# Edge stage of a graph layer: four normalised tiles stored as two interleaved pairs, read at a stride of 8 bytes instead of 16

## Chip, cores and metric

The kernel runs on one core of one Trainium2 chip. The metric is device time in microseconds from start to end of one execution. Before the change it is 1327.7 us, the median of three runs (1327.56 to 1327.87).

## What is computed

One graph layer over 100000 nodes of 160 features (64 scalars, then 32 vectors of 3) and 25000 edges. Cut to what matters:

```python
h = jnp.maximum(_layernorm(x, axis=-1), 0.0)      # normalise, relu
s, v = h[:, :64], h[:, 64:].reshape(N, 32, 3)
skip_s, skip_v = s @ W_skip0, einsum('nmi,mk->nki', v, W_skip1)
s, v = s @ W_nl0, einsum('nmi,mk->nki', v, W_nl1)
w = relu(edge_feature @ W_fc1) @ W_fc2            # 224 weights per edge
xs, xv = s[dst], v[dst]                           # rows of each edge
tp = products of w, xs, xv and the edge's direction
agg = segment_sum(tp, src) / 32
out_s = agg_s @ W_out_s + skip_s;  out_v = agg_v @ W_out_v + skip_v
out = x + concat(silu(out_s[:, :64]), sigmoid(out_s[:, 64:96]) * out_v)
```

## The kernel before, in words

The host stores each node's vector part component by component, so that a row is 64 scalars and three blocks of 32. The program is written per engine, with semaphores between them, in three stages:

1. **Table stage** (about 0 to 195 us): for each tile of 125 edges TensorE counts, and VectorE, ScalarE and GpSimd work out, in which slot of its target block each message will be found.
2. **Edge stage** (about 200 to 600 us): 200 tiles of 125 edges in 50 groups of `GE` = 4. GpSimd gathers the four tiles' rows of `x` (`gathers`, L501) three groups ahead. VectorE takes their statistics (L642), GpSimd the power -1/2 (L508), VectorE the shift (L656). ScalarE normalises (`norm_e`, L1093) from `xg` into `hn`. TensorE transposes `hn` (`turn_rows`, L1334 and L1335), ScalarE copies the result out of PSUM into `ht` (L1150), TensorE multiplies it by the weights (`rows`, L1289 and L1293) and the edge features by theirs (L1386, L1378). VectorE forms the products (`products`, L794 to L818) with a part on GpSimd (L562, L564). TensorE transposes them (`turn`, L1349), ScalarE copies them out (L1138), TensorE projects them (`project`, L1362 to L1366), ScalarE copies the messages out (L1145), VectorE completes them (L827 to L831) and SP stores them.
3. **Node stage** (about 600 us to the end): for each 1024 nodes the normalisation (L1178), transposes (L1411, L1412), skip products (L1419, L1423), the sum of gathered messages (L1433), gates and residual. It has a tile `nn` of its own, which the change does not touch.

**The tile of the change.** `hn` is `[125, 2, 160, 4]` in float32: two buffers, in each 160 features, and innermost the four tiles of a group. So one tile's features lie 16 bytes apart. ScalarE writes a tile at that stride, once per tile. TensorE transposes features 0 to 127 of each tile apart (L1334, four times a group, stride 16 bytes), and the last 32 features of all four tiles together: they lie in 128 neighbouring elements (L1335, once a group, no stride). In a transpose the tile is the stationary operand, the one that the weight load (PEld) reads, and the identity is streamed.

**What the weights have to match.** Row p of `ht[:, c, t]` is feature p of tile t; its product with `wnl_a` (128x128: `W_nl0` in the scalars' place, `W_nl1` twice for two vector components) is done per tile. Row p of `ht[:, c, 4]` is feature 128 + p // 4 of tile p % 4; `wnl_z` has `W_nl1` at rows j, j + 4, ... for tile j.

**The order of work.** Each engine's order is written out by hand in a loop over groups, `round_e(q, b)`. One round of TensorE is:

```python
turn(1); project(0); weights((0, 2)); turn(2); project(1)
weights((1, 3)); turn(3); project(2)
turn_rows(q + 1, 1 - c)      # waits for e_norm, the fourth tile of hn
project(3); turn(0, p + 1, 1 - c); rows(p_x, c); hidden of q + 1
```

and in ScalarE's round the two places where `hn` is written are:

```python
take(1); norm_e(q + 1, (b + 1) % D, range(0, 2))
take(2); put(q - 2, c, 0)    # L1145, waits for project(1)
norm_e(q + 1, (b + 1) % D, range(2, 4)); take(3); copy of w (L1168)
```

`take` is L1138, `put` is L1145. At the start of the program VectorE clears the tiles that hold weights (L609), and then SP issues the loads of all weights one after the other (L404), the first loads of edge features (L414) and of `x` (L427). TensorE waits for the weights before L1273, VectorE at line 735, after the table stage.

Of the kernel before, what the change touches and what calls it, by code (L numbers as in the profile page):

```python
# [6 lines left out]
ACT = mybir.ActivationFunctionType  # L7
# [6 lines left out]
P = 128  # L14
# [3 lines left out]
def gnn_layer(nc, x, src, dst, edge_vec, edge_feat_t, w_skip0, w_skip1, w_nl0, w_nl1,  # L18
# [11 lines left out]
    N, F = x.shape  # L30
    S = w_skip0.shape[0]
    V = w_skip1.shape[0]
    SG = w_skip0.shape[1]
# [5 lines left out]
    ET, NT = src.shape  # L39
    GE = 4  # L40
# [24 lines left out]
    with ExitStack() as ctx:  # L65
        def sb(name, shape, dt=F32):
            return ctx.enter_context(nc.sbuf_tensor(name, shape, dt))

        def sem(name):
            return ctx.enter_context(nc.semaphore(name))  # L70
# [46 lines left out]

        wsk_a = sb("wsk_a", [P, SG + 2 * V])
        wsk_z = sb("wsk_z", [P, 4 * V])
        wnl_a = sb("wnl_a", [P, S + 2 * V])  # L120
        wnl_z = sb("wnl_z", [P, 4 * V])
        wfc1 = sb("wfc1", [2 * EF, 2 * EF])
        wfc2 = sb("wfc2", [2 * EF, W])
# [37 lines left out]
        with ExitStack() as msg_ctx:  # L161
            def sb_msg(name, shape, dt=F32):
                return msg_ctx.enter_context(nc.sbuf_tensor(name, shape, dt))


            dst_g = sb_msg("dst_g", [P, D, GE], I32)
            xg = sb_msg("xg", [P, D, GE, F])
            ef = sb_msg("ef", [2 * EF, 2, 2 * ET])
            e_stat = sb_msg("e_stat", [ET, D, GE, 6])
            e_sum = sb_msg("e_sum", [ET, D, 5, GE])  # L170
            e_rstd = sb_msg("e_rstd", [ET, D, GE])
            e_bias = sb_msg("e_bias", [ET, D, GE])
            hn = sb_msg("hn", [ET, 2, F, GE])
            ht = sb_msg("ht", [P, 2, GE + 1, ET])
            hid = sb_msg("hid", [2 * EF, 2 * ET])
            w_sb = sb_msg("w_sb", [ET, 2, GE, W])
            tp = sb_msg("tp", [ET, 2, GE, 2 * TU])
            xvh = sb_msg("xvh", [ET, GE, 3, V])
            dot = sb_msg("dot", [ET, 2, GE, V])
            w4xv = sb_msg("w4xv", [ET, GE, 3, V])  # L180
            cr_a = sb_msg("cr_a", [ET, GE, 3, V])
            cr_b = sb_msg("cr_b", [ET, GE, 3, V])
            tpt = sb_msg("tpt", [P, 2, 3 * ET])
# [62 lines left out]
        e_t = sem("e_t")  # L246
# [47 lines left out]
        weight_loads = [(wfc2[0:EF, :], w_fc2), (wfc2[EF:2 * EF, :], w_fc2)]  # L294
        for j in range(2):
# [1 line left out]
            weight_loads.append((wfc1[part, part], w_fc1))  # L297
        weight_loads += [(wo_s[:, :], w_out_s), (wo_u[S:2 * S, V:2 * V], w_out_v[0:S, :]),
                         (wo_u[0:2 * V, 0:V], w_out_v[S:S + 2 * V, :]),
                         (wsk_a[0:S, 0:SG], w_skip0), (wnl_a[0:S, 0:S], w_nl0)]  # L300
        for j in range(2):
            weight_loads.append((wo_v[2 * V * j:2 * V * j + 2 * V, V * j:V * j + V], w_out_v[S:S + 2 * V, :]))
            rows = slice(S + V * j, S + V * j + V)
            weight_loads += [(wsk_a[rows, SG + V * j:SG + V * j + V], w_skip1),
                             (wnl_a[rows, S + V * j:S + V * j + V], w_nl1)]
        for j in range(4):
            cols = slice(V * j, V * j + V)
            weight_loads += [(wsk_z[j:P:4, cols], w_skip1), (wnl_z[j:P:4, cols], w_nl1)]

        def wait(eng, s, value):  # L310

            if not (isinstance(value, int) and value <= 0):
                eng.wait_ge(s, value)
# [54 lines left out]
        with ExitStack() as psum_ctx:  # L368
# [9 lines left out]
            p_t = bank[0][:, 0:(GE + 1) * P].rearrange("p (t c) -> p t c", c=P)[:, :, 0:ET]  # L378
# [7 lines left out]
            f_t = bank[3][:, 0:(GE + 1) * P].rearrange("p (t c) -> p t c", c=P)[:, :, 0:ET]  # L386
# [699 lines left out]
            def _(act):  # L1086
                act.wait_ge(s_tab, 1)
                act.activation(vec_r[:], vec_d2[:], ACT.Sqrt).then_inc(s_sqrt, 1)
                def norm_e(q, b, tiles):
                    act.wait_ge(e_ln, q + 1)  # L1090
                    wait(act, e_t, q - 1)
                    for t in tiles:
                        last = act.activation(hn[:, b % 2, :, t], xg[0:ET, b, t, :], ACT.Relu,  # L1093
                                              bias=e_bias[:, b, t:t + 1], scale=e_rstd[:, b, t:t + 1])
                    if GE - 1 in tiles:
                        last.then_inc(e_norm, 1)
# [3 lines left out]
                def tile_b(t, k, q):  # L1100
                    if k % BATCH < BATCH - 1:
                        done, s = (BR - BR // BATCH) * q + k - k // BATCH, (k - k // BATCH) % 2
                        act.wait_ge(b_dec, BR // BATCH * q + k // BATCH + 1)
                        act.activation(off_slot[:, s, :], iota_slot[0:ET, :], ACT.Abs, bias=slot[:, k:k + 1],  # L1104
                                       scale=-1.0).then_inc(b_off, 1)
                        wait(act, b_tab, t - BLOCK + 1)
                        act.wait_ge(b_off, done + 1)
                        r = k % BLOCK
                        act.activation(slot_v[:, r, :], off_slot[:, s, :], ACT.Relu, bias=row_no[:, r:r + 1],
                                       scale=neg_row[:, r:r + 1]).then_inc(b_slot, 1)  # L1110
                    if isinstance(t, int) and t == BR - 1:
                        norm_e(0, 0, range(GE))
                    if isinstance(t, int) and t == NT - BR:
                        act.wait_ge(e_t, 1)
                        act.activation(ht[:, 0, :, :], f_t, ACT.Copy).then_inc(e_ht, 1)
                    if isinstance(t, int) and t == NT - BR + 8:
                        act.wait_ge(e_h1, 1)
                        act.activation(hid[:], f_h, ACT.Relu).then_inc(e_hid, 1)
                    if isinstance(t, int) and t == NT - 3:
                        act.wait_ge(e_w, 1)  # L1120
                        act.activation(w_sb[:, 0, :, :], f_w, ACT.Copy).then_inc(e_wsb, 1)
# [3 lines left out]
                for r in range(2):  # L1125
                    last = act.activation(tab_row[:, r, :], p_tab[r], ACT.Copy, scale=unit_of_slot[:, 0:1])
                last.then_inc(b_rows_sb, 1)

                def round_e(q, b):
# [28 lines left out]
                    if within(q + 1):  # L1158
                        norm_e(q + 1, (b + 1) % D, range(0, 2))
                    take(2)  # L1160
                    put(q - 2, c, 0)
                    if within(q + 1):
                        norm_e(q + 1, (b + 1) % D, range(2, 4))
# [73 lines left out]
            def _(pe):  # L1237
# [22 lines left out]

                idt = ident[0:ET, 0:ET]

                def turn_first():
                    pe.wait_ge(e_norm, 1)
                    for t in range(GE):
                        pe.transpose(f_t[:, t, :], hn[:, 0, 0:P, t], idt)
                    pe.transpose(f_t[:, GE, :], hn[:, 0, P:F, :], idt).then_inc(e_t, 1)

                def hidden_first():
                    pe.wait_ge(s_w, 16 * len(weight_loads))  # L1270
# [15 lines left out]

                def rows(to, c):
                    for t in range(GE):
                        pe.matmul(to[:, t, 0:P], ht[:, c, t, :], wnl_a[:],  # L1289
                                  start=(t % 2 == 0), stop=True, skip_group_check=True)  # L1290
                        if t % 2 == 1:
                            j = t // 2
                            last = pe.matmul(to[:, 2 * j:2 * j + 2, P:F], ht[:, c, GE, :],  # L1293
                                             wnl_z[:, 2 * V * j:2 * V * j + 2 * V],
                                             start=False, stop=True, skip_group_check=True)
                    return last
# [6 lines left out]
                def tile_b(t, k, q):  # L1303
                    if tile_exists(t + 2):
                        pe.wait_ge(b_hot, t + 3)
                    pe.wait_ge(b_rank, t + 1)
                    count(k, tri_rest, k, not tile_exists(t + 2))
                    if tile_exists(t + 2):
                        count(k, ones_h, k + 1)
                        count(k, tri_before, k + 2).then_inc(b_pre, 1)  # L1310
                    if tile_exists(t - BLOCK):
                        table(t - BLOCK, (k - BLOCK) % BR, q if k >= BLOCK else q - 1)
                    if isinstance(t, int) and t == NT - BR:
                        turn_first()
                    if isinstance(t, int) and t == NT - BR + 12:
                        hidden_first()
# [11 lines left out]
                def turn_rows(q, c):  # L1328

                    pe.wait_ge(e_norm, q + 1)  # L1330
                    wait(pe, e_ht, q)
                    wait(pe, e_hid, q)
                    for t in range(GE):
                        pe.transpose(p_t[:, t, :], hn[:, c, 0:P, t], idt)  # L1334
                    pe.transpose(p_t[:, GE, :], hn[:, c, P:F, :], idt).then_inc(e_t, 1)  # L1335

                def round_e(q, b):
                    p, c = q - 2, b % 2
# [179 lines left out]
```

## Time and profile before

| | |
|---|---|
| median of three runs | 1327.7 us |
| lowest, highest | 1327.56, 1327.87 us |
| span of the profiled execution (first to last instruction) | 1322.7 us |
| TensorE matmuls busy | 1197.9 us, 91% |
| TensorE weight loads busy | 998.1 us, 75% |
| VectorE busy | 1099.5 us, 83% |
| ScalarE busy | 1029.0 us, 78% |
| GpSimd busy | 828.6 us, 63% |
| mean granted TensorE clock | 0.978 |

For the profiled execution only its span is given; the median is 5.0 us longer than that span, which is what lies around the first and the last instruction. PE stands for TensorE's matmuls, PEld for its weight loads, which overlap them. A matmul's recorded duration includes its way through the array, so that one record overlaps the next: what one more matmul costs is read from the distance between starts. In a row that merges several instructions, "x4" counts them, and the time beside the start reaches from the first's start to the last's end.

### The profile page before, as it was taken

The numbers are of one execution on the slowest core, as the hardware profiler recorded it, in microseconds if no ns is written. First come the engines' busy times: TensorE is split into PE (matmuls) and PEld (weight loads), VectorE is DVE, ScalarE is ACT, GpSimd is POOL, SyncE is SP. The second block draws the span as 40 slices with busy tenths as digits, with TensorE's granted clock in tenths as the row PEclk, the third lists the DMA queues.
The fourth block names the chain that finished last, engine by engine and source line by source line (L and its number), as shares of the span: only waits on it lengthen the run. The fifth ranks groups of instructions, "written<-read, shape, count | busy, mean of one in ns | idle before, by whom it ended". The sixth has DMA issues, their size and how long they took to land.

```text
span 1322.7 us, 33310 instructions
## 1 busy us (share of the span) xinstructions
PE 1197.9 (91%) x8853; PEld 998.1 (75%) x8853; DVE 1099.5 (83%) x4058; ACT 1029.0 (78%) x2446; POOL 828.6 (63%) x1077
## 2 busy tenths in 40 slices
PE   4899998999999999994999998999889999889986
PEld 2455557888888888883888787888778888778876
DVE  7999998888889888875688788888788888788775
ACT  2777776788878888864888788888888887888884
POOL 5555557787878888712766566566566666566651
PEclk9999997999999999996999999999999999999998
DMA  6000002344434443422888878888878888888873
GB/s 214 8 0 0 0 15 65 105 111 111 112 104 113 112 110 108 113 60 52 218 248 245 251 225 246 248 248 253 238 231 241 253 245 248 239 235 255 241 192 108
DMA packets 90930, 212.40 MB, mean 161 GB/s; under 512 B 15030, under 2 KB 56281, under 8 KB 90878
## 3 DMA queue, kind: packets, MB, share of 16 engines
q1 hardware_dynamic: 62462, 155.23, 35.4%
q0 software_dynamic: 28416, 56.56, 21.0%
q8 instruction: 22, 0.36, 0.1%
q14 instruction: 30, 0.25, 0.1%
HBM read 127.73 MB, written 84.00 MB: 160 GB/s over the span
## 4 chain that ended last, share of the span: by engine, by line
PE 38%; DVE 18%; ACT 9%; issue 9%; DMA 8%; POOL 2%; SPq 0%; DVEq 0%; ACTq 0%; POOLq 0%
DMA xb<-x 7%; PE bank L1419 6%; PE bank L1349 5%; DVE n_stat L858 5%; ACT nn L1178 4%; DVE ob L949 4%; PE bank L1289 4%; PE bank L1378 3%; PE bank L1366 3%; PE bank L1433 3%; PE bank L1362 3%; PE bank L1364 3%; PE bank L1334 2%; PE bank L1411 2%; DVE ob L956 2%
## 5 line engine op out<-in xcount | busy, mean ns | idle before, releaser
L574 POOL DMA_INDIRECT mg<-messages,slot_m x392 | 430.0, 1097 | 274.5 <-issue 107.3
L1178 ACT ACTIVATE nn<-xb,n_bias,n_rstd 128x160 f32<-128x160 f32 x784 | 383.7, 650 | 91.0 <-DVE n_bias L656 91.0
L1419 PE MATMUL bank<-wsk_a,nt 128*128 128x160 f32 x1568 | 298.8, 313 | 58.3 <-DVE ob L949 57.0
L1419 PEld LDWEIGHTS bank<-wsk_a,nt 128*128 128x128 f32 x1568 | 227.2, 192 | 75.7 <-issue 57.2
L501 POOL DMA_INDIRECT xg<-x,dst_g x200 | 208.8, 1044 | 61.4 <-issue 56.1
L858 DVE BATCH_NORM_STATS2 n_stat<-xb 128x6 f32<-128x160 f32 x784 | 203.0, 314 | 29.1 <-DMA xb<-x 28.4
L949 DVE SCALAR_TENSOR_TENSOR ob<-sg,bank 128x128 f32<-128x128 f32 x588 | 131.7, 281 | 100.8 <-ACT ob L1193 100.7
L1433 PE MATMUL bank<-mg,hot 64*128 64x192 f32 x1568 | 181.8, 351 | 4.7 <-DVE hot L934 4.7
L1411 PE MATMUL bank<-ident,nn 128*128 128x128 f32 x784 | 147.8, 312 | 13.7 <-ACT nn L1178 13.7
L1185 ACT ACTIVATE nt<-bank 128x640 f32<-128x640 f32 x196 | 137.5, 702 | 23.2 <-PE bank L1412 18.5
L1411 PEld LDWEIGHTS bank<-ident,nn 128*128 128x128 f32 x784 | 110.1, 209 | 58.1 <-issue 57.4
L956 DVE TENSOR_TENSOR ob<-ob,xb 128x1280 f32<-128x1280 f32 x98 | 146.1, 1491 | 2.6
L1433 PEld LDWEIGHTS bank<-mg,hot 64*128 64x128 f32 x1568 | 123.8, 187 | 18.1 <-DVE hot L934 4.9
L1423 PE MATMUL bank<-wsk_z,nt 128*128 128x64 f32 x784 | 130.8, 249 | 0.0
L1423 PEld LDWEIGHTS bank<-wsk_z,nt 128*128 128x128 f32 x784 | 129.4, 192 | 0.0
L711 DVE CUSTOM_DVE_ANT_0 rank_junk<-bin_hot,bank 125x392 bf16<-125x392 f16 x200 | 110.9, 555 | 3.4 <-PE bank L1246 2.7
L1138 ACT ACTIVATE tpt<-bank 128x375 f32<-128x375 f32 x200 | 98.8, 494 | 16.8 <-PE bank L1349 15.4
L1093 ACT ACTIVATE hn<-xg,e_bias,e_rstd 125x160 f32<-125x160 f32 x200 | 108.9, 652 | 1.2 <-DVE e_bias L656 1.2
L1349 PE MATMUL bank<-ident,tp 125*128 125x125 f32 x600 | 103.5, 281 | 4.6 <-DVE tp L818 3.9
L1349 PEld LDWEIGHTS bank<-ident,tp 125*128 125x128 f32 x600 | 68.5, 145 | 37.1 <-issue 29.4
L1104 ACT ACTIVATE off_slot<-iota_slot,slot 125x128 f32<-125x128 f16 x160 | 62.2, 389 | 39.3 <-POOL slot L534 39.3
L934 DVE TENSOR_TENSOR hot<-iota_local,mg 128x256 f32<-128x256 f32 x196 | 75.9, 419 | 14.8 <-DMA mg<-messages,slot_m 14.8
(187 smaller groups left out, 2476.2 us busy)
## 6 DMA issues: line engine op xcount, KB each, us to landing
xb<-x SPq DMA_DIRECT2D x97, 640.0 KB, 6.9
out_dram<-ob SPq DMA_DIRECT2D x97, 640.0 KB, 3.6
messages<-msg SPq DMA_DIRECT2D x50, 390.6 KB
mg<-messages,slot_m POOLq DMA_INDIRECT x392
ef<-edge_feat_t SPq DMA_DIRECT2D x50, 125.0 KB, 5.9
xg<-x,dst_g POOLq DMA_INDIRECT x200
xb<-x SPq DMA_DIRECT2D x1, 420.0 KB
out_dram<-ob SPq DMA_DIRECT2D x1, 420.0 KB
```

Source lines behind the costliest of these rows:

```text
L501: pool.indirect_dma_start(xg[:, b, t, :], None, x[:, :], bass.IndirectOffsetOnAxis(ap=dst_g[:, b, t:t + 1], axis=0)).then_inc(e_x[b], 16)
L574: pool.indirect_dma_start(mg[:, m, k, :], None, messages[:, :], bass.IndirectOffsetOnAxis(ap=slot_m[:, m, k:k + 1], axis=0)).then_inc(n.g[ ...
L858: done = dve.bn_stats(n_stat[:, u // U, u % U * G + g, :], xb[:, u, g, :])
L949: last = dve.scalar_tensor_tensor(out=o[:, :, S + V * j:S + V * j + V], in0=sg[:, h, :, :], scalar=1.0, in1=z[:, :, part], op0=ALU.add, op ...
L956: dve.tensor_tensor(o, o, xb[:, u, :, :], ALU.add).then_inc(n.res, 1)
L1178: last = act.activation(nn[:, u % 2, h, :, g % 4], xb[:, u, g, :], ACT.Relu, bias=n_bias[:, u // U, c:c + 1], scale=n_rstd[:, u // U, c:c ...
L1185: act.activation(nt[:, h, :], q_t[h], ACT.Relu).then_inc(n.ht, 1)
L1349: last = pe.transpose(p_tt[:, i * ET:(i + 1) * ET], tp[:, c, t, TURN[i]:TURN[i] + P], idt)
L1411: pe.transpose(q_t[h][:, t * P:(t + 1) * P], nn[:, u % 2, h, 0:P, t], ident[:])
L1419: pe.matmul(z[:, t, 0:F], nt[:, h, t * P:(t + 1) * P], wsk_a[:], start=(t % 2 == 0), stop=False, skip_group_check=True)
L1423: pe.matmul(z[:, 2 * j:2 * j + 2, F:Z], nt[:, h, 4 * P:5 * P], wsk_z[:, 2 * V * j:2 * V * j + 2 * V], start=False, stop=every, skip_group_ ...
L1433: last = pe.matmul(q_z[h][:, t, 0:Z], hot[slots, u % 2, pair, :], mg[slots, u % U, pair, 0:Z], start=False, stop=True, skip_group_check=True)
```

## The change

`hn` becomes `[125, 2, 2, 5, 32, 2]`: two buffers; in each a half for tiles 0 and 2 and a half for tiles 1 and 3 (index `t % 2`); five blocks of 32 features; innermost the two tiles of the pair (index `t // 2`). One tile's features then lie 8 bytes apart. In the half of tiles 1 and 3 the five blocks are stored in reverse order, so that the last block of this half is next to the last block of the other: the last 32 features of all four tiles lie in 128 neighbouring elements again and are transposed together. For tiles 1 and 3 the features arrive in `ht` in the order of blocks 3, 2, 1, 0, so `wnl_a` gets a second version with its rows in that order, and the rows of `wnl_z` change places. Four weight loads are added and the memset of `wnl_a` is twice as wide.

```diff
-        wnl_a = sb("wnl_a", [P, S + 2 * V])
+        wnl_a = sb("wnl_a", [P, 2, S + 2 * V])
...
-            hn = sb_msg("hn", [ET, 2, F, GE])
+            hn = sb_msg("hn", [ET, 2, 2, F // V, V, 2])
...
-                         (wsk_a[0:S, 0:SG], w_skip0), (wnl_a[0:S, 0:S], w_nl0)]
+                         (wsk_a[0:S, 0:SG], w_skip0), (wnl_a[0:S, 0, 0:S], w_nl0), (wnl_a[P - S:P - V, 1, 0:S], w_nl0[V:S, :]),
+                         (wnl_a[P - V:P, 1, 0:S], w_nl0[0:V, :])]
...
-                             (wnl_a[rows, S + V * j:S + V * j + V], w_nl1)]
+                             (wnl_a[rows, 0, S + V * j:S + V * j + V], w_nl1),
+                             (wnl_a[V - V * j:2 * V - V * j, 1, S + V * j:S + V * j + V], w_nl1)]
...
-            weight_loads += [(wsk_z[j:P:4, cols], w_skip1), (wnl_z[j:P:4, cols], w_nl1)]
+            weight_loads += [(wsk_z[j:P:4, cols], w_skip1), (wnl_z[j % 2 * 2 * V + j // 2:j % 2 * 2 * V + 2 * V:2, cols], w_nl1)]
...
-                        last = act.activation(hn[:, b % 2, :, t], xg[0:ET, b, t, :], ACT.Relu,
+                        order = slice(None) if t % 2 == 0 else slice(None, None, -1)
+                        last = act.activation(hn[:, b % 2, t % 2, order, :, t // 2], xg[0:ET, b, t, :], ACT.Relu,
                                               bias=e_bias[:, b, t:t + 1], scale=e_rstd[:, b, t:t + 1])
...
+                def turn_tiles(to, c):
+                    flat = hn[:, c, :, :, :, :].rearrange("p j k c i -> p (j k c i)")
+                    for t in range(GE):
+                        begin = t // 2 + (0, 2 * (F + V))[t % 2]
+                        pe.transpose(to[:, t, :], flat[:, begin:begin + 2 * P - 1:2], idt)
+                    return pe.transpose(to[:, GE, :], flat[:, 2 * P:2 * P + 4 * V], idt)
...
-                    for t in range(GE):
-                        pe.transpose(p_t[:, t, :], hn[:, c, 0:P, t], idt)
-                    pe.transpose(p_t[:, GE, :], hn[:, c, P:F, :], idt).then_inc(e_t, 1)
+                    turn_tiles(p_t, c).then_inc(e_t, 1)
...
-                        pe.matmul(to[:, t, 0:P], ht[:, c, t, :], wnl_a[:],
+                        pe.matmul(to[:, t, 0:P], ht[:, c, t, :], wnl_a[:, t % 2, :],
```

No instruction of TensorE, VectorE or GpSimd changes its place. What the four instructions of a group look like on ScalarE, where tile 1 and tile 3 are now written in two dimensions; the first group before:

```order
L1093 ACTIVATE hn<-xg,e_bias,e_rstd 125x160 x4
```

and with the change:

```order
L1096 ACTIVATE hn<-xg,e_bias,e_rstd 125x160
L1096 ACTIVATE hn<-xg,e_bias,e_rstd 125x5x32
L1096 ACTIVATE hn<-xg,e_bias,e_rstd 125x160
L1096 ACTIVATE hn<-xg,e_bias,e_rstd 125x5x32
```

Their number and order are the same. On SP's queue, at the start of the program, the piece with the loads into `wnl_a`, before:

```order
L404 DMA wnl_a<-W_nl 64x64
L404 DMA wo_v<-W_out_v 64x32
L404 DMA wsk_a<-W_skip 32x32
L404 DMA wnl_a<-W_nl 32x32
L404 DMA wo_v<-W_out_v 64x32
L404 DMA wsk_a<-W_skip 32x32
L404 DMA wnl_a<-W_nl 32x32
```

and with the change:

```order
L406 DMA wnl_a<-W_nl 64x64
L406 DMA wnl_a<-W_nl 32x64 x2
L406 DMA wo_v<-W_out_v 64x32
L406 DMA wsk_a<-W_skip 32x32
L406 DMA wnl_a<-W_nl 32x32 x2
L406 DMA wo_v<-W_out_v 64x32
L406 DMA wsk_a<-W_skip 32x32
L406 DMA wnl_a<-W_nl 32x32 x2
```

Four loads are added; everything behind them on this queue comes four issues later.

## Rows read from the trace of the kernel before

**Rows 1.** The page: busy time, share and instructions of each engine.

```profile
PE 1197.9 (91%) x8853; PEld 998.1 (75%) x8853; DVE 1099.5 (83%) x4058; ACT 1029.0 (78%) x2446; POOL 828.6 (63%) x1077
```

**Rows 2.** Busy time by stretch, edge stage and transition to the node stage.

```profile
core 0: us, PE busy (x) PEld busy (x) DVE busy (x) ACT busy (x) POOL busy (x), PEclk, DMA share, GB/s
500.00:550.00 50.00, 49.86 (x410) 44.31 (x410) 43.43 (x164) 41.05 (x85) 40.43 (x46) 1.00 0.41 113
...
600.00:620.00 20.00, 5.90 (x22) 4.94 (x22) 12.94 (x66) 9.91 (x23) 3.44 (x4) 0.57 0.17 43
620.00:660.00 40.00, 34.20 (x238) 30.58 (x238) 23.21 (x84) 28.27 (x72) 29.49 (x29) 0.87 0.76 189
```

**Rows 3.** Timeline of ScalarE in one round: start, us, engine, line.

```profile
305.10 0.54 ACT L1145 ACTIVATE msg<-bank 125x448 f32<-125x448 f32 x1
305.54 1.09 ACT L1093 ACTIVATE hn<-xg,e_bias,e_rstd 125x160 f32<-125x160 f32 x2
306.43 0.51 ACT L1138 ACTIVATE tpt<-bank 128x375 f32<-128x375 f32 x1
```

**Rows 4.** Timeline of TensorE's weight loads and matmuls in the same round.

```profile
306.68 0.56 PEld L1334 LDWEIGHTS bank<-ident,hn 125*128 125x128 f32 x4
...
306.34 0.38 PE L1366 MATMUL bank<-wo_u,tpt 128*125 128x64 f32 x2
306.69 0.75 PE L1334 MATMUL bank<-ident,hn 125*128 125x125 f32 x4
307.27 0.27 PE L1335 MATMUL bank<-ident,hn 125*128 125x125 f32 x1
...
307.98 0.49 PE L1349 MATMUL bank<-ident,tp 125*128 125x125 f32 x3
308.31 0.60 PE L1289 MATMUL bank<-wnl_a,ht 128*125 128x128 f32 x4
```

**Rows 5.** Timeline, the next round: ScalarE's last two writes, TensorE's matmuls.

```profile
313.35 1.09 ACT L1093 ACTIVATE hn<-xg,e_bias,e_rstd 125x160 f32<-125x160 f32 x2
...
314.06 0.38 PE L1366 MATMUL bank<-wo_u,tpt 128*125 128x64 f32 x2
314.48 0.75 PE L1334 MATMUL bank<-ident,hn 125*128 125x125 f32 x4
```

**Rows 6.** Timeline of TensorE where three transposes without stride follow a wait.

```profile
593.53 0.54 PE L1349 MATMUL bank<-ident,tp 125*128 125x125 f32 x3 [0.68 <-ACT tpt L1138]
593.91 0.36 PE L1362 MATMUL bank<-wo_s,tpt 96*125 96x96 f32 x2
```

**Rows 7.** Groups of weight loads, 260 to 540 us: busy us, mean ns, idle before.

```profile
L1349 PEld LDWEIGHTS bank<-ident,tp 125*128 125x128 f32 x432 | 49.2, 145 | 23.4 <-issue 20.2
...
L1289 PEld LDWEIGHTS bank<-wnl_a,ht 128*125 128x125 f32 x288 | 37.2, 188 | 0.0
...
L1334 PEld LDWEIGHTS bank<-ident,hn 125*128 125x128 f32 x148 | 20.8, 211 | 5.4 <-ACT hn L1093 3.3
...
L1335 PEld LDWEIGHTS bank<-ident,hn 125*128 125x128 f32 x37 | 5.8, 156 | 0.0
```

**Rows 8.** One line, L1334: duration ns min/median/max, first and last start.

```profile
L1334 PEld LDWEIGHTS bank<-ident,hn x196: 195/216/231, 200.3 to 578.4; 125*128 125x128 f32 x196
```

**Rows 9.** Groups of ScalarE, whole program.

```profile
L1093 ACT ACTIVATE hn<-xg,e_bias,e_rstd 125x160 f32<-125x160 f32 x200 | 108.9, 652 | 1.2 <-DVE e_bias L656 1.2
...
L1109 ACT ACTIVATE slot_v<-off_slot,row_no,neg_row 125x128 f16<-125x128 f32 x160 | 78.9, 493 | 6.8
...
L1145 ACT ACTIVATE msg<-bank 125x448 f32<-125x448 f32 x100 | 54.5, 545 | 10.3 <-PE bank L1366 6.5
...
L1168 ACT ACTIVATE w_sb<-bank 125x896 f32<-125x896 f32 x49 | 44.0, 898 | 0.1
```

**Rows 10.** Timeline of ScalarE in the table stage.

```profile
99.53 0.49 ACT L1109 ACTIVATE slot_v<-off_slot,row_no,neg_row 125x128 f16<-125x128 f32 x1
99.93 0.38 ACT L1104 ACTIVATE off_slot<-iota_slot,slot 125x128 f32<-125x128 f16 x1
```

**Rows 11.** Waits, 260 to 540 us (36 rounds): us in total, times, longest.

```profile
ACT hid L1156 <- PE bank L1386: 40.6, 36, 1.2
DVE hu L827 <- ACT msg L1145: 25.4, 33, 0.9
...
POOL cr_a L562 <- DVE w4xv L794: 13.2, 32, 0.9
```

**Rows 12.** Timeline of SP's queue and of VectorE at the start; the weights' first reader.

```profile
15.99 0.59 SPq L404 DMA_DIRECT2D wnl_z<-W_nl  x1
...
1.44 0.17 DVE L609 MEMSET wnl_a<- 128x128 f32 x1
...
7.13 0.38 DVE L620 COPY dst_g<-dst_i 128x4 int32<-128x4 int32 x4 [4.46 <-DMA dst_i<-dst]
...
L1273 PEld LDWEIGHTS bank<-ef,wfc x2: 190/191/192, 184.0 to 184.2; 128*128 128x128 f32 x2
```

More of the change, by code:

```diff
@@ L1261, in _ @@
                 idt = ident[0:ET, 0:ET]
+                def turn_tiles(to, c):
[4 more added lines that the diff above has]
+                    return pe.transpose(to[:, GE, :], flat[:, 2 * P:2 * P + 4 * V], idt)
                 def turn_first():
                     pe.wait_ge(e_norm, 1)
-                    for t in range(GE):
-                        pe.transpose(f_t[:, t, :], hn[:, 0, 0:P, t], idt)
-                    pe.transpose(f_t[:, GE, :], hn[:, 0, P:F, :], idt).then_inc(e_t, 1)
+                    turn_tiles(f_t, 0).then_inc(e_t, 1)
                 def hidden_first():
@@ L1332, in turn_rows @@
                     wait(pe, e_hid, q)
-                    for t in range(GE):
-                        pe.transpose(p_t[:, t, :], hn[:, c, 0:P, t], idt)
-                    pe.transpose(p_t[:, GE, :], hn[:, c, P:F, :], idt).then_inc(e_t, 1)
+                    turn_tiles(p_t, c).then_inc(e_t, 1)
                 def round_e(q, b):
```

## The prediction

> **What bounds the kernel now.** I read the shares first: TensorE has matmuls under way 91% of the span [rows 1], but that is a mean over three stages, and only the middle one changes. The busy times by stretch come next: in the edge stage TensorE is busy 49.86 of 50 us, VectorE 43.4, ScalarE 41.1, GpSimd 40.4, at a granted clock of 1.00 [rows 2]. A reader should not stop at "TensorE is full": a matmul's record overlaps its successor, so a short stall does not show as idle time. The starts in the timeline show it. The last L1366 before the row transposes starts about 0.11 us after the first of its pair (306.34 + 0.38 less one duration of 0.27 is 306.45), and the weight load of L1334 starts only at 306.68 [rows 4], where neighbours without a wait follow at about 0.11 us. What it waits for is in the row of ScalarE: two writes of `hn` start at 305.54 and end 1.09 us later, at 306.63 [rows 3], 0.05 us before the load. One round on, the pair ends at 314.44 and L1334 starts at 314.48, there 0.31 us after the last L1366 (314.17) [rows 5]. So TensorE loses 0.13 to 0.2 us a round to the last tile of `hn`, and the chain of a round is: `project(1)` on TensorE, L1145, two writes of `hn`, the transposes, the rest of TensorE's round. Both things that the change touches, the write and the read of `hn`, lie on it, in series. The number of rounds is 196 / 4 = 49 [rows 8]; one more group is transposed in the table stage.
>
> **The reads.** Before: from the start of the first strided transpose to the start of L1335 is 307.27 - 306.69 = 0.58 us for four [rows 4]. Three transposes without stride after a wait take 593.91 - 593.53 = 0.38 us [rows 6], and each further one 0.11 (from 307.98 to 308.31 is 0.33 for three [rows 4]): 0.49 us for four. So a read with no penalty saves 0.09 us a round, and a read that stays as slow saves 0. The cause is the weight load: 211 ns for L1334 against 156 for L1335 and 145 for L1349, the same size without stride [rows 7]. How much does 8 bytes give back? No row has that stride. But the load of L1289 takes 188 ns and its successors still follow at about the unstrided distance, so a load need not reach 145 ns to be hidden; if the penalty goes with the number of 16-byte pieces touched (128 before, 64 now, 32 without stride), the load would take about 211 - 2/3 x 60 = 171 ns, under 188. I take the full 0.09: 49 x 0.09 = 4.4 us. The bounds are 0 and 49 x 0.09 = 4.4 us.
>
> The trace says that a stride of 16 bytes costs 55 to 66 ns a load. The Trainium skill (SBUF — State Buffer, in the note on cachelines) says both that two hits in a 16-byte line are needed for full bandwidth and that float32 may be strided by 4 elements for free. By the second sentence the reads would already be free, the change would bring 0, and L1334 should be as fast as L1335; the rows disagree. By the first, 8 bytes is free.
>
> **The writes.** The two writes behind L1145 take 1.09 us together [rows 3]; the next instruction starts at 306.43, 0.20 before their end, whereas ScalarE's L1109 in the table stage, also with a scale and a bias read from SBUF and without stride, has its successor start 0.40 after it and ends 0.09 after that, at 0.493 [rows 9, 10]. The strided write has a long tail. L1109 has 128 elements; per further element the group L1168 against L1145 gives (898 - 545) / 448 = 0.8 ns [rows 9], so 32 more are 0.025 us. A pair without stride would take (0.40 + 0.025) + (0.493 + 0.025) = 0.94 us, 0.15 less. The bounds are therefore 0 and 0.15 us a round. With half of the pieces touched, of which the unstrided write would touch a quarter, I take two thirds: 0.10 us, 49 x 0.10 = 4.9 us. It comes off whole: TensorE's wait is 0.13 to 0.2 us longer than nothing, and the reads' saving lies behind it. The writes of tiles 0 and 1 are off the path; ScalarE waits 1.13 us a round for L1386 (40.6 / 36) [rows 11], and their saving lengthens that wait. The two-dimensional form of tiles 1 and 3 I cost at nothing.
>
> **What comes for nothing.** Four more loads on SP's queue at 0.42 to 0.6 us put what is behind them back by some 2.2 us. The last weight load is issued at 16.0 us and the first reader is at 184 us [rows 12]; that cover is 167 us long, and the same holds for the loads of edge features and `x` behind them. The memset of `wnl_a` is 128 columns wider, about one more of 0.17 us; VectorE then waits 4.46 us for `dst` [rows 12]. Without that cover it would cost 0.17 us once. The products with the second `wnl_a` stream as many columns as before: 0.
>
> **Who is late next.** After 0.19 us less a round TensorE's wait for `hn` is about 0.03 to 0.1 us. GpSimd has 13.2 / 36 = 0.37 us a round of waiting before L562, VectorE 25.4 / 36 = 0.7 before L827 [rows 11]. Both are more than 0.19, so neither becomes the bound. Behind the edge stage nothing changes but its start. In the transition the granted clock is 0.57 and 0.87 in the two stretches [rows 2], so parts of it run at 1.2 GHz; where these parts fall may shift with the start, and I allow 1.5 us either way.
>
> **Sum.** 4.4 + 4.9 = 9.3 us: the span goes from 1322.7 to 1313.4 us, and the median, 5.0 us longer than the span, from 1327.7 to 1318.4 us. About 0.2% (2.7 us) is what a measurement can tell from no change.
>
> **Rivals.**
> 1. *Only the reads gain.* If a write with gaps is slow whatever the gap, the tail stays: 1327.7 - 4.4 = 1323.3 us. For it: reader and writer are different engines, and no row shows a float32 write at 8 bytes. Against it: the same 16-byte gap costs on both. Chance 0.22.
> 2. *No gain at all.* Any gap over 4 bytes may cost the same, for both: 1327.7 us. For it: the trace has only the two ends of the scale. The second sentence of the cachelines note of the Trainium skill (SBUF — State Buffer) also gives this time, by a free read before and after; the rows on the loads speak against that way to it. The Trainium skill (GPSIMD Engine Reference, performance pitfalls) puts the cliff of another engine's SBUF reads above 8 bytes; no run here shows it, and carried over to these engines it would rule this rival out. Chance 0.12.
> 3. *Slower, through tile 3.* The wait ends with tile 3, one of the two that are written as five blocks, last block first. If jumping back between blocks costs on ScalarE, TensorE starts later. The price: the tail of 0.20 us [rows 3] doubled, less the reads' 0.09, is +0.11 us a round, 49 x 0.11 = +5.4: 1333.1 us. It decides from a write that is 0.09 us longer, and is measurable from 0.145. Against it: the group has only five blocks, 0.02 us for each would be needed. Chance 0.06.
> 4. *Another engine takes the place of the wait*, GpSimd with its 0.37 us first: if its round stretches as VectorE's instructions come closer to its own, half of the gain is kept: 1323 us. Chance 0.05.
>
> **How the numbers follow.** The forecast has 0.55. Its own range is from all of both terms, 49 x (0.09 + 0.15) = 11.8, with 1.5 for the transition (1314.4), to half of the writes' term less 1.5 (1322). With rivals 1 and 4 and their 1.5 us or a weaker read the range is 1314.4 to 1325.7 us and leaves out rivals 2 and 3, 0.18. Faster: 0.55 + 0.22 + 0.05 = 0.82; same 0.12; slower 0.06.
>
> **What would show it.** Weight loads of the strided transposes at 145 to 180 ns instead of 211, and 0.49 us instead of 0.58 from the start of the first of the four to the start of the fifth. The pair of writes at about 0.99 us instead of 1.09, with tile 1's and tile 3's form no longer than the others. The distance from the last L1366 to the first transpose shorter by 0.10 us, and a round of 7.60 instead of 7.79 us (from L1334 at 306.69 to L1334 at 314.48 [rows 4, 5]). The edge stage ends 9 us earlier and the node stage lasts as long as before. It is wrong if the writes' durations stay at 650 ns, if the five-block form is longer, or if the node stage gives the time back.

## The result, and the profile after

The changed kernel takes 1318.6 us (median of seven runs, 1316.24 to 1320.59) against 1327.6 us for the kernel before, run beside it (1323.23 to 1331.44). The ratio is 0.9936, with a 95% interval of 0.9919 to 0.9953: faster by 6 to 11 us. The forecast was 1318.4. The total is right; the way to it, as the rows show, is half right. Here and below the ratio with its interval is the one on record; it is not the quotient of the two medians beside it and differs from that by up to 0.4%.

The busy times by stretch of the changed kernel (columns as in [rows 2]), cut where the third and the last group's row transposes start:

```profile
0.00:218.00 218.00, 184.88 (x901) 103.96 (x901) 201.63 (x763) 145.85 (x352) 120.66 (x369) 0.95 0.12 40
218.00:572.00 354.00, 351.35 (x2900) 314.20 (x2899) 317.38 (x1148) 277.62 (x599) 275.30 (x313) 1.00 0.40 109
572.00:1316.00 744.00, 657.22 (x5058) 579.73 (x5057) 582.14 (x2148) 592.58 (x1497) 430.10 (x396) 0.98 0.77 222
```

and the same three pieces of the kernel before:

```profile
0.00:217.00 217.00, 183.20 (x902) 102.81 (x902) 201.07 (x763) 146.47 (x353) 120.53 (x369) 0.95 0.12 40
217.00:578.00 361.00, 357.74 (x2901) 315.88 (x2899) 316.50 (x1148) 290.43 (x600) 276.15 (x313) 1.00 0.39 107
578.00:1322.00 744.00, 656.92 (x5055) 579.44 (x5053) 581.92 (x2148) 592.14 (x1497) 431.95 (x396) 0.98 0.78 222
```

All of the gain is in the middle piece, 361 to 354 us over the same 46 rounds with the same number of instructions. The piece ahead is 1 us longer, the node stage is the same. In the middle piece ScalarE did 13 us less (290.4 to 277.6), weight loads only 1.7 us less: that already points at the writes. The span fell by 5.9 us, from 1322.7 to 1316.8.

The groups of ScalarE and of the weight loads between 260 and 540 us in the changed kernel (count, busy us, mean ns, idle before), which answer to [rows 7, 9]:

```profile
L1096 ACT ACTIVATE hn<-xg,e_bias,e_rstd 125x160 f32<-125x160 f32 x148 | 69.3, 524 | 0.0
...
L1355 PEld LDWEIGHTS bank<-ident,tp 125*128 125x128 f32 x442 | 50.5, 145 | 23.9 <-issue 20.5
...
L1270 PEld LDWEIGHTS bank<-ident,hn 125*128 125x128 f32 x148 | 20.5, 209 | 0.5
L1271 PEld LDWEIGHTS bank<-ident,hn 125*128 125x128 f32 x37 | 5.7, 154 | 0.0
```

A write of `hn` fell from 652 to 524 ns. A strided weight load fell from 211 to 209: a stride of 8 bytes is as slow to read as one of 16. The timeline of one round of the changed kernel, in place of [rows 3, 4]:

```profile
305.27 0.93 ACT L1096 ACTIVATE hn<-xg,e_bias,e_rstd 125x160 f32<-125x160 f32 x2
306.09 0.46 ACT L1141 ACTIVATE tpt<-bank 128x375 f32<-128x375 f32 x1
...
306.06 0.38 PE L1372 MATMUL bank<-wo_u,tpt 128*125 128x64 f32 x2
306.28 0.72 PE L1270 MATMUL bank<-ident,hn 125*128 125x125 f32 x4
306.83 0.27 PE L1271 MATMUL bank<-ident,hn 125*128 125x125 f32 x1
...
306.25 0.55 PEld L1270 LDWEIGHTS bank<-ident,hn 125*128 125x128 f32 x4
```

The pair of writes takes 0.93 us where it took 1.09 and ends at 306.20. The first load still starts 0.05 us behind it, so the load still waits for the last tile. The matmul behind it no longer does: the first L1270 starts 306.28 - 306.17 = 0.11 us after the last L1372, the distance that the prediction took for neighbours without a wait, where it was 306.69 - 306.45 = 0.24 before. In every second round of the middle of the stage 0.17 us is left, where it was 0.32. So the shorter writes have taken away nearly all of this wait: 0.06 us of it is left, in every second round. From the first of the four transposes to the fifth it is 306.83 - 306.28 = 0.55 us, 0.58 before; the runs below show whether that is the read.

### The profile page after: what moved, and what is told of

The parts are those of the page before. It is cut to its first block, busy times and chain, and to the rows that moved or that the text cites. A ratio compares the mean times of both kernels' runs of the same rounds, so it can differ in the third digit from the quotient of the medians.

```text
span 1316.8 us, 33314 instructions
## 1 busy us (share of the span) xinstructions
PE 1193.4 (91%) x8853; PEld 997.9 (76%) x8853; DVE 1101.2 (84%) x4058; ACT 1016.0 (77%) x2446; POOL 826.1 (63%) x1077
## 4 chain that ended last, share of the span: by engine, by line
PE 40%; DVE 18%; DMA 9%; issue 8%; ACT 7%; POOL 2%; SPq 1%; DVEq 0%; ACTq 0%; POOLq 0%
DMA xb<-x 8%; PE bank L1425 6%; PE bank L1355 6%; DVE n_stat L860 5%; DVE ob L951 4%; ACT nn L1181 4%; PE bank L1384 4%; PE bank L1297 4%; PE bank L1372 3%; PE bank L1368 3%; PE bank L1370 3%; PE bank L1439 3%; PE bank L1270 2%; PE bank L1417 2%; DVE ob L958 2%
## 5 line engine op out<-in xcount | busy, mean ns | idle before, releaser
L860 DVE BATCH_NORM_STATS2 n_stat<-xb 128x6 f32<-128x160 f32 x784 | 202.0, 312 | 29.3 <-DMA xb<-x 28.5
L1141 ACT ACTIVATE tpt<-bank 128x375 f32<-128x375 f32 x200 | 96.6, 483 | 24.6 <-PE bank L1355 24.5
L1096 ACT ACTIVATE hn<-xg,e_bias,e_rstd 125x160 f32<-125x160 f32 x200 | 93.2, 523 | 1.3 <-DVE e_bias L658 1.2
```

Of the source, the lines that this page charges most:

```text
L860: done = dve.bn_stats(n_stat[:, u // U, u % U * G + g, :], xb[:, u, g, :])
```

## The experiments

All distances between rounds below are taken at the end of the edge stage, between the starts of the last two groups' transposes: 7.71 us in the kernel before and 7.56 us in the changed one. In the middle of the stage rounds of 7.72 and 7.80 us alternate before the change and rounds of 7.56 and 7.64 with it: the same 0.15 to 0.16 us less.

The runs beside which the kernel before took 1452 or 1477 us instead of 1327 (called disturbed below) have to be read by such rounds alone. There ScalarE stood still for up to 3 us at a time for something that the profile calls remote, most rounds took 8 to 13 us, and only two or three of the last five are free of it. ScalarE's waits from 300 to 600 us of the first such run (us in total, times, longest); the traces of the runs that took about 1320 us have no such row:

```profile
ACT ht L1153 <- remote: 28.9, 15, 2.8
...
ACT msg L1148 <- remote: 17.4, 17, 1.5
```

The anchors, weight loads of the last two groups, of the kernel before:

```profile
570.38 0.56 PEld L1334 LDWEIGHTS bank<-ident,hn 125*128 125x128 f32 x4
578.09 0.56 PEld L1334 LDWEIGHTS bank<-ident,hn 125*128 125x128 f32 x4
```

and of the changed kernel:

```profile
564.72 0.56 PEld L1270 LDWEIGHTS bank<-ident,hn 125*128 125x128 f32 x4
572.28 0.56 PEld L1270 LDWEIGHTS bank<-ident,hn 125*128 125x128 f32 x4
```

### Writes and reads apart

The theory after the result (W): all of the gain is the write; reads at 8 bytes bring nothing. The rival (R) is the split that was predicted. Four kernels keep one side and change the other.

**Writes at 8 bytes, reads at 16.**

```diff
-                        pe.transpose(to[:, t, :], flat[:, begin:begin + 2 * P - 1:2], idt)
+                        pe.transpose(to[:, t, :], flat[:, t:t + 4 * P - 3:4], idt)
```

> The writes of the changed kernel (8 bytes), but the four transposes of a group read at a stride of 16 bytes (the wrong elements, so the output differs). Theory W (all of the gain is the write): last write of hn 0.52 us, round 7.60 us and total as the changed kernel, 0.994 of before. Rival R (as predicted, reads give 0.09 a round): from the first transpose to the fifth longer than in the changed kernel and half of the gain gone, 0.997 of before.

```profile
637.26 0.56 PEld L1270 LDWEIGHTS bank<-ident,hn 125*128 125x128 f32 x4
644.83 0.56 PEld L1270 LDWEIGHTS bank<-ident,hn 125*128 125x128 f32 x4
```

A round of 7.57 us, that of the changed kernel: going back to reads at 16 bytes costs 0.01 us at most. That is theory W. The matmuls of the first of these two groups say the same:

```profile
637.29 0.73 PE L1270 MATMUL bank<-ident,hn 125*128 125x125 f32 x4
637.85 0.27 PE L1271 MATMUL bank<-ident,hn 125*128 125x125 f32 x1
```

With reads at 16 bytes the first transpose starts 0.56 us ahead of the fifth, with reads at 8 bytes 0.55 to 0.56; so most of the fall from 0.58 came with the shorter wait. The total does not fit either theory: 1458.7 against 1452.4 us, ratio 1.0061 (1.0022 to 1.0101).

**Writes at 16 bytes, reads at 8.** The kernel before, with `hn[:, c, :, :]` read as one run:

```diff
-                        pe.transpose(p_t[:, t, :], hn[:, c, 0:P, t], idt)
+                        pe.transpose(p_t[:, t, :], hn[:, c, :, :].rearrange("p f t -> p (f t)")[:, t:t + 2 * P - 1:2], idt)
```

> The writes of the kernel before (16 bytes), the four transposes of a group read at 8 bytes (the wrong elements, so the output differs). Theory W: weight load of the transposes 212 ns, last write 0.63 us, round 7.76 us, total 1.000 of before. Rival R: weight load about 170 ns or less, round 7.67 us, total 0.997 of before.

```profile
636.15 0.55 PEld L1334 LDWEIGHTS bank<-ident,hn 125*128 125x128 f32 x4
643.86 0.55 PEld L1334 LDWEIGHTS bank<-ident,hn 125*128 125x128 f32 x4
```

A round of 7.71 us, as before the change; the median load is 209 ns, the median write 648 ns. The read's part of the change is worth nothing. The total, 1450.4 against 1452.4 us, ratio 1.0009 (0.9982 to 1.0036), agrees with W, in a batch where W's other half did not show.

**Writes at 8 bytes, reads without a stride** (`flat[:, t * P:t * P + P]`).

> The writes of the changed kernel, the four transposes read neighbouring elements (the wrong ones, so the output differs). Both theories: weight load 145 to 156 ns, from the first transpose to the fifth 0.49 instead of 0.58 us, round 7.51 us, total 4 us under the changed kernel, 0.991 of before. A third view, that the load's length depends on something other than the stride: still 212 ns.

```profile
634.99 0.41 PEld L1270 LDWEIGHTS bank<-ident,hn 125*128 125x128 f32 x4
642.46 0.42 PEld L1270 LDWEIGHTS bank<-ident,hn 125*128 125x128 f32 x4
```

The four loads take 0.41 instead of 0.56 us (median 141 ns), and the round is 7.47 us, 0.09 less than at 8 bytes. The price of a strided read was sized rightly in the prediction, but 8 bytes give none of it back. The total, 1458.0 us, ratio 1.0059 (1.0027 to 1.0092), again is not what was expected (0.991).

**Writes at 16 bytes, reads without a stride.** The same read in the kernel before.

> The writes of the kernel before, the four transposes read neighbouring elements (the wrong ones, so the output differs). Weight load 145 to 156 ns, 0.49 us from the first transpose to the fifth, last write still 0.63 us, round 7.67 us instead of 7.76: the two parts add up.

```profile
640.65 0.41 PEld L1334 LDWEIGHTS bank<-ident,hn 125*128 125x128 f32 x4
648.27 0.41 PEld L1334 LDWEIGHTS bank<-ident,hn 125*128 125x128 f32 x4
```

7.62 us (the one run took 1457.7 us). The four corners are 7.71 (16 and 16), 7.62 (16 and none), 7.56 (8 and 8), 7.47 (8 and none): the write is worth 0.15 us, a read without a stride 0.09, and they add up, as two stations in series do. The two corners without a stride and the two mixed runs rest on two or three free rounds of one disturbed execution each, which agree to 0.02 us.

### How the times go with the stride

**No stride at all**: `hn` as `[125, 2, 4, 160, 1]`, with the shared transpose of the last features replaced by one of tile 3.

```diff
-            hn = sb_msg("hn", [ET, 2, F, GE])
+            hn = sb_msg("hn", [ET, 2, GE, F, 1])
...
-                        last = act.activation(hn[:, b % 2, :, t], xg[0:ET, b, t, :], ACT.Relu,
+                        last = act.activation(hn[:, b % 2, t, :, 0], xg[0:ET, b, t, :], ACT.Relu,
...
-                        pe.transpose(p_t[:, t, :], hn[:, c, 0:P, t], idt)
-                    pe.transpose(p_t[:, GE, :], hn[:, c, P:F, :], idt).then_inc(e_t, 1)
+                        pe.transpose(p_t[:, t, :], hn[:, c, t, 0:P, 0], idt)
+                    pe.transpose(p_t[:, GE, :], hn[:, c, 3, 0:P, 0], idt).then_inc(e_t, 1)
```

> Each tile of hn by itself without a stride, written and read at 4 bytes; the transpose of the last 32 features of four tiles reads 128 features of tile 3 in their place, so the output differs. Theory W (a write is slow only over 8 bytes): writes 0.52 us as at 8. Rival (the time goes with the pieces touched, two thirds were given back): writes 0.45 to 0.49 us. Reads: 145 to 156 ns.

**12 bytes**: the same with `F, 3`; here the fifth transpose is read at 12 bytes too.

> As the run without a stride, but with 12 bytes between elements of hn, written and read, and the same transpose replaced. If the write's limit lies between 8 and 12 bytes: about 0.65 us as at 16. If the time goes with the 16-byte lines touched: between 0.52 and 0.65. Reads: 212 ns if any stride costs the same.

The writes and loads of the line, without a stride (min/median/max in ns):

```profile
L1093 ACT ACTIVATE hn<-xg,e_bias,e_rstd x200: 503/510/522, 42.8 to 566.3; 125x160 f32<-125x160 f32 x100
...
L1334 PEld LDWEIGHTS bank<-ident,hn x196: 138/139/231, 199.7 to 567.1; 125*128 125x128 f32 x196
```

and at 12 bytes:

```profile
L1093 ACT ACTIVATE hn<-xg,e_bias,e_rstd x200: 563/591/619, 41.6 to 571.8; 125x160 f32<-125x160 f32 x100
...
L1334 PEld LDWEIGHTS bank<-ident,hn x196: 188/201/231, 198.7 to 572.8; 125*128 125x128 f32 x196
```

The median write takes 510, 522, 591 and 654 ns at 4, 8, 12 and 16 bytes. From 4 to 8 bytes nearly nothing, then about 65 ns for each further 4 bytes. At 8 bytes W's view held (a write is slow only above 8), and the one by which two thirds were given back fell. At 12 bytes there is no jump: the value lies halfway between those at 8 and at 16, and so do the rounds, 7.61 us between 7.56 and 7.71. The loads take 139, 212, 201 and 216 ns: the whole penalty is there at 8 bytes, and 12 is no worse. The Trainium skill (SBUF — State Buffer, the note on cachelines) wants two hits in a 16-byte line for full bandwidth; ScalarE's writes agree (8 bytes has two, and costs 12 ns of a possible 144), the weight loads of TensorE do not (8 bytes has two, and costs 73 of a possible 77 ns). Its sentence that float32 may be strided by 4 elements for free agrees with neither.

The run without a stride took 1316.8 us and the one at 12 bytes 1318.7 us (one each), both undisturbed. The first has rounds of 7.45 us, 0.11 less than the changed kernel, which fits the 0.09 for a read without a stride. It is hardly faster in all: its node stage, from the last group's transposes on, lasts 748.0 us where the changed kernel's lasts 744.5, and a single run can't tell 2 us.

### Does the backward write cost?

```diff
-                        order = slice(None) if t % 2 == 0 else slice(None, None, -1)
+                        order = slice(None)
```

> The changed kernel, but tiles 1 and 3 are written forwards, as one run of 160 (their blocks land in the wrong order, so the output differs). Theory W: durations of tiles 1 and 3 as with the five blocks backwards, 0.52 us, round 7.60 us. Rival (jumping back costs): tiles 1 and 3 shorter than 0.51 us, round shorter by the difference.

```profile
L1096 ACT ACTIVATE hn<-xg,e_bias,e_rstd x200: 511/523/542, 43.1 to 570.8; 125x160 f32<-125x160 f32 x100
```

and in the changed kernel:

```profile
L1096 ACT ACTIVATE hn<-xg,e_bias,e_rstd x200: 509/522/542, 43.6 to 571.7; 125x160 f32<-125x160 f32 x100
```

No difference in the median, and rounds of 7.56 us in both. The five blocks in reverse order are free. The one run took 1323.4 us, 3 us more than the slowest of the changed kernel; since the last group's transposes start at the same time to 1 us in both traces, that is not the edge stage.

### The same layout in the node stage

`nn`, `wsk_a` and `wsk_z` get the treatment of `hn`, `wnl_a` and `wnl_z`; everything is computed.

```diff
-        nn = sb("nn", [P, 2, 2, F, 4])
+        nn = sb("nn", [P, 2, 2, 2, F // V, V, 2])
...
-                            last = act.activation(nn[:, u % 2, h, :, g % 4], xb[:, u, g, :], ACT.Relu,
+                            order = slice(None) if g % 2 == 0 else slice(None, None, -1)
+                            last = act.activation(nn[:, u % 2, h, g % 2, order, :, g % 4 // 2], xb[:, u, g, :], ACT.Relu,
...
-                            pe.matmul(z[:, t, 0:F], nt[:, h, t * P:(t + 1) * P], wsk_a[:], start=(t % 2 == 0),
+                            pe.matmul(z[:, t, 0:F], nt[:, h, t * P:(t + 1) * P], wsk_a[:, t % 2, :], start=(t % 2 == 0),
```

> The changed kernel with the same two interleaved pairs in the node stage (nn, wsk_a, wsk_z), everything computed. Theory W: the 784 writes of nn take 520 instead of 650 ns, start to start about 0.41 instead of 0.43 us. Where ScalarE or the wait for nn ends the chain (ACT nn has 4% of the chain before) this gives 5 to 20 us: total 0.98 to 0.99 of before. Rival: the node stage is bound by the products and by DMA, the shorter write ends in idle time of ScalarE, total as the changed kernel, 0.994.

Groups from 640 to 1300 us, with the layout in both stages:

```profile
L1184 ACT ACTIVATE nn<-xb,n_bias,n_rstd 128x160 f32<-128x160 f32 x746 | 329.2, 527 | 78.6 <-DVE n_bias L660 78.6
L1191 ACT ACTIVATE nt<-bank 128x640 f32<-128x640 f32 x187 | 131.3, 702 | 25.2 <-PE bank L1423 24.5 <-issue 0.7
...
L862 DVE BATCH_NORM_STATS2 n_stat<-xb 128x6 f32<-128x160 f32 x712 | 184.1, 313 | 40.0 <-DMA xb<-x 39.8
```

and of the changed kernel:

```profile
L1181 ACT ACTIVATE nn<-xb,n_bias,n_rstd 128x160 f32<-128x160 f32 x752 | 368.8, 651 | 80.2 <-DVE n_bias L658 80.2
L1188 ACT ACTIVATE nt<-bank 128x640 f32<-128x640 f32 x187 | 131.4, 703 | 22.0 <-PE bank L1418 17.6 <-issue 0.3
...
L860 DVE BATCH_NORM_STATS2 n_stat<-xb 128x6 f32<-128x160 f32 x712 | 183.8, 313 | 29.3 <-DMA xb<-x 28.5
```

1319.7 against 1326.6 us, ratio 0.9930 (0.9906 to 0.9954), beside 0.9936 for the change alone: no gain can be seen, though the two intervals leave room for some 4 us either way. I had expected 5 to 20 us more by theory W, and that was wrong. The writes are shorter by the same 124 ns (651 to 527), and ScalarE saves 40 us of work, but the wait of VectorE for loads of `x` grows from 28.5 to 39.8 us and ScalarE's wait for the transposes from 17.6 to 24.5. The last write's end is not waited for here. In the changed kernel:

```profile
900.29 1.98 ACT L1181 ACTIVATE nn<-xb,n_bias,n_rstd 128x160 f32<-128x160 f32 x4
...
904.99 0.56 PEld L1417 LDWEIGHTS bank<-ident,nn 128*128 128x128 f32 x4 [0.23 <-issue]
```

The four writes end at 902.27, 2.72 us before the first load that reads them; in 194 of the 196 groups that distance is over 0.5 us, where it is 0.05 us in the edge stage. The same shorter write is worth 7 us in the stage where its end is waited for in every round, and nothing that can be measured in the one where it is not. That was the rival's forecast for the time.

### Taking the write off the path

If only the end of the last write matters, writing `hn` earlier must make both layouts equal. ScalarE waits 1.1 us a round ahead of the copy of the hidden layer [rows 11]; the first pair goes there, the second behind `take(1)`:

```diff
                     take(0)
+                    if within(q + 1):
+                        norm_e(q + 1, (b + 1) % D, range(0, 2))
...
                     take(1)
                     if within(q + 1):
-                        norm_e(q + 1, (b + 1) % D, range(0, 2))
+                        norm_e(q + 1, (b + 1) % D, range(2, 4))
                     take(2)
                     put(q - 2, c, 0)
-                    if within(q + 1):
-                        norm_e(q + 1, (b + 1) % D, range(2, 4))
```

> The changed kernel, everything computed, with both pairs of writes of hn earlier in ScalarE's round: the first before the copy of the hidden layer, where ScalarE waits 1.1 us, the second before the third copy of tpt. Theory W (after the change TensorE still waits 0.08 to 0.16 us a round for the last write, and its first transpose starts cold): L1270 follows L1372 at about 0.11 us, round 7.4 us instead of 7.6, 5 to 10 us under the changed kernel, 0.987 to 0.99 of before. Rival: GpSimd or VectorE takes over (GpSimd has 0.23 us a round left), round 7.5 to 7.6 us, total at most 3 us under the changed kernel.

> The kernel before (16 bytes, everything computed) with the same earlier writes. Theory W: the write is off the path, so its 0.65 us no longer matter and the time is that of the changed kernel with the same order, within 2 us, though the weight loads take 211 ns. Rival (the layout itself helps, by the reads or by less traffic): 5 us or more slower than the changed kernel with the same order.

Loads of the last two groups, with the changed layout:

```profile
645.13 0.59 PEld L1270 LDWEIGHTS bank<-ident,hn 125*128 125x128 f32 x4
652.65 0.59 PEld L1270 LDWEIGHTS bank<-ident,hn 125*128 125x128 f32 x4
```

and with the layout before:

```profile
647.01 0.60 PEld L1334 LDWEIGHTS bank<-ident,hn 125*128 125x128 f32 x4
654.53 0.60 PEld L1334 LDWEIGHTS bank<-ident,hn 125*128 125x128 f32 x4
```

7.52 us in both, though a write's median is 530 ns in the one and 658 in the other. In the free rounds the layout helps through the write's end and through nothing else. The size was off, though. I expected 7.4 us, since a wait of 0.08 to 0.16 us and a cold start should go. TensorE's matmuls in the same round show what is left:

```profile
652.54 0.38 PE L1372 MATMUL bank<-wo_u,tpt 128*125 128x64 f32 x2
652.76 0.68 PE L1270 MATMUL bank<-ident,hn 125*128 125x125 f32 x4
653.27 0.27 PE L1271 MATMUL bank<-ident,hn 125*128 125x125 f32 x1
```

and in the last round of the changed kernel:

```profile
572.09 0.38 PE L1372 MATMUL bank<-wo_u,tpt 128*125 128x64 f32 x2
572.31 0.72 PE L1270 MATMUL bank<-ident,hn 125*128 125x125 f32 x4
572.87 0.27 PE L1271 MATMUL bank<-ident,hn 125*128 125x125 f32 x1
```

The first L1270 starts 0.22 us after the first L1372 in both. I had taken the wait of the load, 0.08 us, for a wait of the matmul; there was none left in these rounds. What went is 0.05 us between the first and the fifth transpose (0.51 instead of 0.56), since the loads no longer start late. A round of 7.52 us lies in the range of the rival by which GpSimd or VectorE takes over, but nothing of what the matmuls gained here was lost to another engine. The totals were 1477.3 us (ratio 1.0025, 0.9994 to 1.0056) for the changed layout and 1487.9 us (1.0113, 1.0059 to 1.0167) for the one before, both beside a kernel before of 1477 us. By these totals the rival's sign was met: the layout before is 10 us slower than the changed one with the same order, and the two intervals do not overlap. The free rounds do not show where these 10 us arise, and the trace kept of the slower one is that of its fastest execution (1473.7 us). So what the layout does in disturbed rounds is open. No undisturbed time of the earlier writes is known, and no version is shown to beat the changed kernel.

### The two halves once more

> The same kernel as w8_r16 once more, since the chip there took 1452 us for the kernel before: writes at 8, reads at 16 bytes, output differs. Theory W: 0.994 of before. Rival R: 0.997.

> The same kernel as w16_r8 once more: writes at 16, reads at 8 bytes, output differs. Theory W: 1.000 of before. Rival R: 0.997.

ScalarE stood still as in the first batch: 1482.4 against 1477.2 us, ratio 1.0060 (1.0019 to 1.0100), and 1478.2, ratio 1.0018 (0.9984 to 1.0052). Neither total tells the theories apart. The rounds repeat the first batch: 7.57 us for writes at 8 bytes and 7.71 us for writes at 16.

## Why the prediction came out

**What bounds the kernel**: right. In the kernel before the first strided load starts 0.05 us behind the end of the last write in every round, and the matmul behind it 0.24 to 0.33 us after the last L1366, where 0.11 is the distance without a wait.

**The reads**: wrong. "I take the full 0.09", by the count of 16-byte pieces, was the step that failed: a load takes 209 ns at 8 bytes, not 171, and four of them save 0.00 to 0.01 us. The bound below, 0, was the value. What a read without a stride would give, 0.09 us, was sized rightly.

**The writes**: right in kind, too small. The upper bound, 0.15 us for the pair, was the value (from 1.09 to 0.93 in the timeline, 0.16), where two thirds of it was taken. The reason given, pieces touched, is wrong as well: 8 bytes is nearly as good as none. "It comes off whole" held, but with nothing to spare: the shortening is as large as the wait of 0.13 to 0.2 us that it had to fit into.

**The sum**: 0.09 + 0.10 = 0.19 us a round was predicted, 0 + 0.15 measured. Two errors of opposite sign cancelled in part: 49 x 0.15 = 7.4 us, against 7 us measured in the middle piece, 5.9 in the span and 9.0 between the medians, whose interval reaches from 6 to 11. The prediction's round of 7.79 us is of the longer kind that alternates with a shorter one; that kind fell to 7.64 us and not to 7.60.

Two more errors cancelled in the last step. The span was forecast at 1313.4 us and measured at 1316.8. And the 5.0 us between the median and the span of before are not what lies around the first and the last instruction: in the profiled execution of every later run the time is only 1.8 to 1.9 us longer than the span (1318.67 and 1316.8 in the changed kernel). The profiled execution of before by this took about 1324.6 us, less than its median. The span came out 3.4 us over the forecast, the difference 3.1 us under it. That 1318.6 stands so near to 1318.4 is luck.

The range's upper end, 1325.7 us, follows from no sum in the prediction; rivals 1 and 4 with their 1.5 us end at 1324.8.

**What comes for nothing, and who is late next**: right as far as seen. The four loads at the start and the wider memset have no reader near them; the piece ahead of the edge stage is 1 us longer, but hardly by them: the kernel with the layout in both stages loads still more weights and reaches its third group at 216.1 us, where the kernel before does at 217.2 and the changed one at 218.2. GpSimd's wait ahead of `cr_a` fell from 13.2 us in 36 rounds to 8.5 in 37 and is not gone. The node stage neither gained nor lost.

**The rivals**: 1 (only the reads gain) is the reverse of what happened; 2 (none) fell with the writes; 3 (tile 3 backwards) is refuted by the forward run; 4 (another engine takes over) did not show, since the whole of the writes' term arrived in the rounds.

What stays open: in the batches in which ScalarE stands still, the writes at 8 bytes with ScalarE's order unchanged came out 0.6% slower in all three measurements, though the free rounds are shorter; with the earlier writes it was the 16-byte layout that came out slower. No run tells why, and so the cause given here is shown for undisturbed rounds only.

## What to carry to other kernels

Price a strided operand on both its sides, and separately: the engine that writes it and the engine that reads it have different limits, and here the change named the reads and was paid for by the writes. An access is worth shortening where its end is what somebody waits for in every round, and no further than that wait reaches: the same 0.13 us a write was worth 7 us in one stage and nothing in the other. Read a wait from the starts of the matmuls and not only from those of the weight loads: a load 0.08 us late held no matmul back. And where one term comes from an assumed law between two known ends, measure a point between them, or keep the ends as the forecast's own range.

## What was not expected of the hardware

ScalarE's write of 160 float32 elements takes 510, 522, 591 and 654 ns at strides of 4, 8, 12 and 16 bytes, while TensorE's load of 128 float32 columns takes 139, 212, 201 and 216 ns: for the one 8 bytes is almost free, for the other it already costs everything. In the transposes the load's 70 ns show only in part: between rounds four of them take 0.09 us more in all. In two of the batches the same program took 9 to 11% longer (1452 and 1477 instead of 1327 us), with ScalarE idle for up to 3 us at a time.
